# Attention keys split once and stored compactly; scores from four part products, 256 columns a pass

## The chip, the cores and the metric

The kernel runs on one core of a Trainium2 chip. The metric is the device time of one execution in microseconds. Engines: TensorE (PE, and PEld for its weight loads), VectorE (DVE), ScalarE (ACT), GpSimd (POOL) and SyncE (SP), which here only issues DMAs.

## What is computed

A residual stream `x` of 16 batches x 128 tokens x 256 passes through two blocks, each with a cross-attention to `ctx_2048` (same shape) and a feed-forward, each weighted by the tanh of a gate and fed by a layernorm without weights:

```python
x = x + tanh(g_xattn[0]) * L0_xattn(ctx, ctx, layernorm(x), ssm_kernel, D, 8)
x = x + tanh(g_ffn[0]) * L0_ffn(layernorm(x), ...)     # 8 shared units, 8 routed experts, top 2
x = x + tanh(g_xattn[1]) * L1_xattn(layernorm(x), ctx, ctx)
x = x + tanh(g_ffn[1]) * L1_ffn(layernorm(x), ...)     # 2 shared units, 32 routed experts, top 6
```

The change touches the third line. `L1_xattn` is causal softmax attention in each batch of 128 tokens, with 16 heads of 16 dimensions, scores `q k^T / 4`, and keys and values that are both slices of `ctx_2048`. All of it is fp32 in the reference.

## The kernel before

The program has four stages, and each engine has its own instruction queue that runs through them in order: `ctx` (the first cross-attention, a convolution), `f0` (the first feed-forward), `att` (the attention) and `f1` (the second feed-forward). Semaphores are set and awaited by hand.

**Precision.** TensorE runs most products in fp32r, a rounded fp32. Where more is needed an operand is split into a high part (a ScalarE copy that rounds) and a low part (the rest, a subtraction on VectorE or GpSimd), and the product is the sum of part products.

**Feed-forward (`feed_forward`, L167).** Two passes over the units, in half blocks of 512 tokens: K counts unit and half, 64 steps in `f0` (K < 16 shared, 16 to 31 routed, 32 to 47 shared, 48 to 63 routed). `h_prod(K + 1)` is 12 matmuls of 512 columns, `o_prod(K)` 6. Between them lie: hidden activation (ScalarE), the product with the gate rows of routed units (VectorE, L520) and with the second half (L525), `y_hi` (ScalarE, L444) and `y_lo` (VectorE, L308). SP runs its own loop over K in `sync`: `weights(K/2 + 4)` waits until unit K/2's weights are split, `gate_rows(K)` loads a row of gates to all partitions and waits until the slot of four routed steps before is free. At K = NK - 16 = 48 it calls `attention_loads` (6 key blocks, two constants, 2 value blocks). Over the last 12 steps `attention_ahead_act`, `_pe` and `_pool` prepare the first queries and keys.

**Attention.** A step n of 64 is a group of four heads: batch b = n // 4, group t = n % 4. The keys of a group are prepared on the host as a block diagonal of 128 rows x 512 columns (four heads, each 16 rows twice, and 128 keys), almost all of it zeros, in `k_blk`. `load_keys` brings one in (128 rows of 2 KB, ring of 6), `key_hi` and `key_lo` split it (ScalarE, GpSimd; ring of 4). Queries: `query_normed` normalizes a batch, `query_hi` and `query_lo` split it into `xn_split`, laid out so that one 128 x 128 transpose gives 64 rows of high and 64 rows of low parts of four heads; `query_turned` does four transposes (t = 3, for batch b + 2), `query_copy` scales and copies them to `q_split_t` (t = 0). `scores(n)` is three passes of 512 columns into one bank: the causal mask in bf16, query parts x high key block, query parts x low key block. VectorE takes the maxima (`maxima`) and subtracts them (`shifted`); `turned(n)` transposes the four heads (four transposes); ScalarE takes the exponential (`probs`); `values(n)` multiplies by the values with a column of ones. After each batch: `out_copy` (ScalarE), `out_rows` (four transposes, at t = 2 of the next), then `inverse`, `scaled`, `residual`, `moments` on VectorE.

TensorE's order in a step n (`c_tensor`) is `turned(n)`, `scores(n + 2)`, `values(n)`, then whatever is due. ScalarE's (`c_scalar`) is `out_copy` at t = 0, `probs(n)`, `query_copy` at t = 0, `key_hi(n + 4)`, `query_normed` at t = 2, `query_hi` at t = 3. GpSimd's (`c_gpsimd`): `key_lo(n + 4)`, `query_lo` at t = 3, and at n = 4 and 40 the `rstd` of the next norm. SP's (`c_sync`): the keys from n = 6 on, and behind the keys of n = 4m the values of batch m, which wait for `values` of step 4m - 5.

## Time and profile before

| | us |
|---|---|
| median of 3 runs (936.82 to 937.28) | 937.21 |
| profiled execution, its own time | 935.47 |
| its span, first to last instruction | 933.6 |
| PE busy | 898.5 (96%) |
| DVE busy | 603.4 (65%) |
| ACT busy | 551.0 (59%) |
| POOL busy | 202.4 (22%) |
| mean granted TensorE clock | 0.99 |

The chain of work that ended last is 88% TensorE: 37% the first products and 28% the second products of the feed-forwards (L646, L682). The attention lies between about 402 and 537 us. Times in rows are from the start of the span. A busy TensorE is not one at its peak, since the ends of its matmuls are modelled.

### The profile page before, as it was taken

Reading aid. Unit: us, or ns where it says so; the run is one execution under the profiler, and the core shown is the slowest. Engines: PE = TensorE matmul, PEld = TensorE weight load, DVE = VectorE, ACT = ScalarE, POOL = GpSimd, SP = SyncE. Lnnn points to the kernel's source line nnn. Section 1 sums busy time; section 2 is a strip of 40 time slices with the busy share of each in tenths; the row PEclk is TensorE's granted clock in tenths of the full one; section 3 lists DMA queues with packets and bytes.
Section 4 is the critical chain, followed back from the end, with each engine's and each line's share of the span. In section 5 each row is a group of like instructions: output and inputs, shape, how many; then the busy total and the mean of one; then the engine's idle time right before and its main releaser. Section 6 shows DMA issues by size and latency. Waiting matters only on the chain.

```text
span 933.6 us, 13901 instructions
## 1 busy us (share of the span) xinstructions
PE 898.5 (96%) x4704; PEld 719.5 (77%) x4704; DVE 603.4 (65%) x1390; ACT 551.0 (59%) x955; POOL 202.4 (22%) x172
## 2 busy tenths in 40 slices
PE   5899899999999999989999989999999999999998
PEld 5798788777788888856666667777788888888886
DVE  6678664465564566588888776566855466656654
ACT  3222343434444335468889677677777877777774
POOL 5899320000000012147777530000000000000000
PEclk9799999999999999999999999999999999999999
DMA  9101020333311351215554315434444244444443
GB/s 301 68 2 68 7 62 1 109 108 91 96 51 39 114 173 66 59 57 170 170 170 167 117 30 169 131 125 142 137 142 139 93 136 140 154 147 136 152 128 104
DMA packets 57957, 104.36 MB, mean 112 GB/s; under 512 B 7296, under 2 KB 13824, under 8 KB 57504
## 3 DMA queue, kind: packets, MB, share of 16 engines
q1 hardware_dynamic: 57168, 103.34, 34.5%
q8 instruction: 38, 0.62, 0.3%
q14 instruction: 31, 0.25, 0.1%
q10 hardware_dynamic: 720, 0.14, 0.1%
HBM read 101.03 MB, written 2.42 MB: 111 GB/s over the span
## 4 chain that ended last, share of the span: by engine, by line
PE 88%; DVE 5%; ACT 2%; POOL 1%; issue 1%; DMA 1%; SPq 1%; DVEq 0%; ACTq 0%; POOLq 0%
PE bank L646 37%; PE bank L682 28%; PE bank L1426 3%; PE bank L1437 2%; PE bank L1111 2%; PE bank L1113 2%; PE bank L1114 2%; PE bank L1126 2%; PE bank L1419 1%; PE bank L1418 1%; PE bank L350 1%; PE bank L1414 1%; PE bank L332 1%; DMA toeplitz<-in_kpad 1%; PE bank L1446 1%
## 5 line engine op out<-in xcount | busy, mean ns | idle before, releaser
L444 ACT ACTIVATE y_hi<-y 128x512 fp32r<-128x512 f32 x200 | 124.1, 621 | 82.2 <-DVE y L525 81.6
L539 DVE TENSOR_TENSOR y<-y,gate_rows 128x512 f32<-128x512 f32 x124 | 85.7, 691 | 120.6 <-ACT y L433 118.2
L682 PE MATMUL bank<-y_hi,w_hi 128*128 128x512 f32 x400 | 157.0, 393 | 1.5 <-DVE y_lo L308 1.0
L682 PE MATMUL bank<-y_lo,w_hi 128*128 128x512 f32 x400 | 156.5, 391 | 0.0
L682 PE MATMUL bank<-y_hi,w_lo 128*128 128x512 f32 x400 | 155.9, 390 | 0.0
L308 DVE TENSOR_TENSOR y_lo<-y,y_hi 128x512 fp32r<-128x512 f32 x196 | 134.3, 686 | 30.0 <-ACT y_hi L444 29.6
L427 ACT ACTIVATE activated<-bank 128x512 f32<-128x512 f32 x136 | 81.3, 597 | 80.9 <-PE bank L646 76.2
L646 PE MATMUL bank<-x_hi_first,w_hi 128*128 128x512 f32 x264 | 106.2, 402 | 0.7 <-DVE w_lo L303 0.7
L646 PE MATMUL bank<-x_hi_first,w_lo 128*128 128x512 f32 x264 | 104.2, 395 | 0.0
L646 PE MATMUL bank<-x_lo_first,w_hi 128*128 128x512 f32 x264 | 104.1, 394 | 0.0
L646 PE MATMUL bank<-x_hi_last,w_hi 128*128 128x512 f32 x264 | 103.9, 394 | 0.0
L646 PE MATMUL bank<-x_hi_last,w_lo 128*128 128x512 f32 x264 | 102.9, 390 | 0.0
L646 PE MATMUL bank<-x_lo_last,w_hi 128*128 128x512 f32 x264 | 102.7, 389 | 0.0
L1303 POOL TENSOR_TENSOR k_blocks_lo<-k_blocks_sb,k_blocks_hi 128x512 fp32r<-128x512 f32 x64 | 82.0, 1282 | 59.5 <-ACT k_blocks_hi L1299 59.0
L682 PEld LDWEIGHTS bank<-y_hi,w_hi 128*128 128x128 f32 x400 | 75.0, 188 | 20.4 <-DVE y_lo L308 2.9
L433 ACT ACTIVATE y<-activated 128x512 f32<-128x512 f32 x136 | 86.0, 632 | 4.3
L682 PEld LDWEIGHTS bank<-y_hi,w_lo 128*128 128x128 f32 x400 | 75.1, 188 | 16.3
L682 PEld LDWEIGHTS bank<-y_lo,w_hi 128*128 128x128 f32 x400 | 75.1, 188 | 16.2
L425 ACT ACTIVATE activated<-bank 128x512 f32<-128x512 f32 x64 | 38.3, 598 | 78.8 <-PE bank L646 78.8
L303 DVE TENSOR_TENSOR w_lo<-w_raw,w_hi 128x512 fp32r<-128x512 f32 (+1 forms) x96 | 75.1, 782 | 10.8 <-ACT w_hi L299 4.9
L299 ACT ACTIVATE w_hi<-w_raw 128x512 fp32r<-128x512 f32 (+1 forms) x100 | 69.7, 697 | 12.5 <-PE bank L682 12.5
L646 PEld LDWEIGHTS bank<-x_hi_first,w_hi 128*128 128x128 f32 x264 | 49.5, 188 | 12.5 <-DVE w_lo L303 1.0
(153 smaller groups left out, 1474.2 us busy)
## 6 DMA issues: line engine op xcount, KB each, us to landing
gate_rows<-gates SPq DMA_DIRECT2D x156, 256.0 KB, 3.7
w_raw<-in_wu SPq DMA_DIRECT2D x68, 256.0 KB, 2.6
k_blocks_sb<-in_k_blk SPq DMA_DIRECT2D x64, 256.0 KB, 4.2
w_raw<-in_wu SPq DMA_DIRECT2D x32, 384.0 KB, 3.1
v_slot<-in_v_rows SPq DMA_DIRECT2D x16, 256.0 KB, 2.6
ctx_windows<-in_ctx_win SPq DMA_DIRECT2D x3, 1024.0 KB, 11.8
toeplitz<-in_kpad SPq DMA_DIRECT2D x4, 512.0 KB, 8.7
X<-in_x SPq DMA_DIRECT2D x4, 512.0 KB, 9.2
```

The source lines that it names most:

```text
L299: act.activation(mem.whi[:, Nu % S, 0:WC], mem.wraw[:, Nu % S, 0:WC], ACT.Copy).then_inc(s_wh, 1)
L303: eng.tensor_tensor(mem.wlo[:, Nu % S, 0:WC], mem.wraw[:, Nu % S, 0:WC], mem.whi[:, Nu % S, 0:WC].bitcast(F32), ALU.subtract).then_inc(s_w ...
L308: eng.tensor_tensor(mem.ylo[:, K % S, :], mem.y[:, K % S, :], mem.yhi[:, K % S, :].bitcast(F32), ALU.subtract).then_inc(s_yl, 1)
L425: act.activation(mem.r[:, K % S, :], bk(2 * K % 3), ACT.Silu).then_inc(s_ac, 1)
L427: act.activation(mem.r[:, K % S, :], bk(K % 3), ACT.Relu).then_inc(s_ac, 1)
L433: act.activation(mem.y[:, K % S, :], mem.r[:, K % S, :], ACT.Square).then_inc(s_sq, 1)
L444: act.activation(mem.yhi[:, K % S, :], mem.y[:, K % S, :], ACT.Copy).then_inc(s_yh, 1)
L539: dve.tensor_tensor(mem.y[:, K % S, :], mem.y[:, K % S, :], gate, ALU.mult).then_inc(s_yd, 1)
L646: last = pe.matmul(o, w_[:, Nu % S, wc], x_[p][:, c, xs], start=(m == 0), stop=(m == 5))
L682: last = pe.matmul(acc(s)[:, c, :], w_[:, Nu % S, wc], y_[:, K % S, :], start=(n == 0 and m == 0), stop=(n == U - 1 and m == 2), skip_grou ...
L1303: pool.tensor_tensor(K2[:, n % KR, :], KM[:, n % KLR, :], K1[:, n % KR, :].bitcast(F32), ALU.subtract).then_inc(s_k2, 1)
L1426: last = pe.transpose(turn_bank(n)[:, g * P:(g + 1) * P], Ds[:, n % DR, g, :], ident[:])
```

## The change

Keys no longer come as zero-padded blocks. The host gives them compactly (`k_rows`: a batch is 128 rows x 256 columns). During `f0`, eight times (two batches at a time) `load_raw` brings them into the value buffer (SP, at K = 16, 18, then behind each store), `split_hi` (ScalarE, K = 19, 22 ... 40) and `split_lo` (GpSimd) split them into `xn_split`'s buffer, and `store_parts` (SP, K = 21, 24 ... 42) writes both parts with four DMAs to an internal DRAM tensor `k_parts`: for each batch 8 groups of 16 high and 16 low rows, each with two heads side by side (256 columns of 4 bytes).

For the attention a ring of 8 blocks (128 x 512) is cleared once on GpSimd (`blocks_zeroed`). `load_keys(n)` fills the two diagonal quarters of a block: for each half, one DMA reads 32 rows of `k_parts` twice (a step of 0 over a count of 2) into 64 partitions x 1 KB. The key blocks are used as they come; `key_hi` and `key_lo` are gone from the attention.

The query split is laid out with each high part and each low part twice, so that a head has 64 rows (high, high, low, low against high, low, high, low of the key), and 128 rows hold two heads. A batch therefore needs eight transposes in two groups (`query_turned(b, a)`, now of fp32r data with an fp32r identity, at t = 3 and at the next t = 0) and two `query_copy`, each placed ahead of `probs` at t = 0 and t = 1. `scores(n)` is the causal pass and two passes of 256 columns. In `f0`'s last steps there are four query groups instead of two, at K = 52, 55, 58, 61, and copies at K = 54, 57, 60, 63.

```diff
-                    if not final and K == NK - 16:
-                        attention_loads(sp)
+                    if not final:
+                        if K in (16, 18):
+                            load_raw(sp, (K - 16) // 2)
+                        if 21 <= K < 45 and K % 3 == 0:
+                            i = (K - 21) // 3
+                            store_parts(sp, i)
+                            if i + 2 < NB // 2:
+                                load_raw(sp, i + 2)
+                        if K == NK - 16:
+                            attention_loads(sp)
...
+                    for i in range(NB // 2):
+                        split_lo(pool, i)
+                    blocks_zeroed(pool)
...
+                        if 19 <= K < 43 and K % 3 == 1:
+                            split_hi(act, (K - 19) // 3)
                         attention_ahead_act(act, NK - K)
...
-        KLR, KR, SR, DR, PR = 6, 4, 3, 3, 3
+        KR, SR, DR, PR = 8, 3, 3, 3
         NQ = 4 * NB
         causal = sb("causal", [P, 4, P], BF16)
         identb = sb("identb", [P, P], BF16)
-        KM = sb("k_blocks_sb", [P, KLR, 4 * P])
-        K1 = sb("k_blocks_hi", [P, KR, 4 * P], F32R)
-        K2 = sb("k_blocks_lo", [P, KR, 4 * P], F32R)
+        K1 = sb("k_blocks", [P, KR, 4 * P], F32R)
+        ident_r = sb("ident_r", [P, P], F32R)
+        xc = sb("xn_c", [P, 2, D])
         V = sb("v_slot", [P, 2, NH1, 32])
-        xc = sb("xn_c", [P, 2, D])
-        xs = sb("xn_split", [P, 2, 4, 2, 64], F32R)
-        Q1 = sb("q_split_t", [P, 2, 4, P], F32R)
+        xs = sb("xn_split", [P, 2, 4, 2, P], F32R)
+        Q1 = sb("q_split_t", [P, 2, 2, 4, P], F32R)
...
+        def split_places(i):
+            parts = xs[:, i % 2].rearrange("p t a f -> p (t a f)")
+            return V[:, i % 2].rearrange("p h d -> p (h d)"), parts[:, 0:2 * D], parts[:, 2 * D:4 * D]
+
+        def load_raw(sp, i):
+            if i >= 2:
+                sp.wait_ge(s_k2, i - 1)
+            sp.dma_start(split_places(i)[0].rearrange("p (b f) -> p b f", b=2),
+                         k_rows[2 * i:2 * i + 2].rearrange("b p f -> p b f")).then_inc(s_kr[i % 2], 16)
+
+        def split_hi(act, i):
+            act.wait_ge(s_kr[i % 2], 16 * (i // 2 + 1))
+            if i >= 2:
+                act.wait_ge(s_ks[i % 2], 64 * (i // 2))
+            raw, high, _ = split_places(i)
+            act.activation(high, raw, ACT.Copy).then_inc(s_k1, 1)
+
+        def split_lo(pool, i):
+            pool.wait_ge(s_k1, i + 1)
+            raw, high, low = split_places(i)
+            pool.tensor_tensor(low, raw, high.bitcast(F32), ALU.subtract).then_inc(s_k2, 1)
+
+        def store_parts(sp, i):
+            sp.wait_ge(s_k1, i + 1)
+            sp.wait_ge(s_k2, i + 1)
+            for part, rows in enumerate(split_places(i)[1:]):
+                for j in range(2):
+                    place = k_parts[2 * i + j].rearrange("(g s d) f -> g s d f", s=2, d=HD1)[:, part]
+                    sp.dma_start(place, rows[:, j * D:(j + 1) * D].bitcast(F32)).then_inc(s_ks[i % 2], 16)
+
+        def blocks_zeroed(pool):
+            pool.memset(K1[:].rearrange("p n f -> p (n f)").bitcast(F32), 0.0).then_inc(s_kz, 1)
+
         def load_keys(sp, n):
-            if n >= KLR:
-                sp.wait_ge(s_k2, n - KLR + 1)
-            sp.dma_start(KM[:, n % KLR, :], k_blk[n]).then_inc(s_kl[n % KLR], 16)
+            if n >= KR:
+                sp.wait_ge(s_s, n - KR + 1)
+            for hh in range(2):
+                first = k_parts.offset + (2 * P * (n // 4) + 64 * (n % 4) + 32 * hh) * D
+                place = bass.AP(k_parts.tensor, first, [[0, 2], [D, 2 * HD1], [1, D]])
+                sp.dma_start(K1[64 * hh:64 * hh + 64, n % KR, hh * D:hh * D + D].bitcast(F32), place).then_inc(s_kl[n % KR], 16)
...
-        def key_hi(act, n):
-            act.wait_ge(s_kl[n % KLR], LOADED + 16 * (n // KLR + 1))
-            if n >= KR:
-                act.wait_ge(s_s, n - KR + 1)
-            act.activation(K1[:, n % KR, :], KM[:, n % KLR, :], ACT.Copy).then_inc(s_k1, 1)
-
-        def key_lo(pool, n):
-            pool.wait_ge(s_k1, n + 1)
-            pool.tensor_tensor(K2[:, n % KR, :], KM[:, n % KLR, :], K1[:, n % KR, :].bitcast(F32),
-                               ALU.subtract).then_inc(s_k2, 1)
...
         def query_hi(act, b):
             act.wait_ge(s_n, b + 1)
             if b >= 2:
-                act.wait_ge(s_xt, b - 1)
-            act.activation(xs[:, b % 2, :, 0, :], xc[:, b % 2, :].rearrange("p (q f) -> p q f", q=4),
-                           ACT.Copy).then_inc(s_hi, 1)
+                act.wait_ge(s_xt, 2 * (b - 1))
+            else:
+                act.wait_ge(s_ks[b], 64 * (NB // 4))
+            act.activation(part_rows(b, 0), copies_of(xc[:, b % 2, :]), ACT.Copy).then_inc(s_hi, 1)
 
         def query_lo(pool, b):
             pool.wait_ge(s_hi, b + 1)
-            pool.tensor_tensor(xs[:, b % 2, :, 1, :], xc[:, b % 2, :].rearrange("p (q f) -> p q f", q=4),
-                               xs[:, b % 2, :, 0, :].bitcast(F32), ALU.subtract).then_inc(s_lo, 1)
-
-        def query_turned(pe, b):
+            pool.tensor_tensor(part_rows(b, 1), copies_of(xc[:, b % 2, :]), part_rows(b, 0).bitcast(F32),
+                               ALU.subtract).then_inc(s_lo, 1)
+
+        def query_turned(pe, b, a):
+            if b + a == 0:
+                pe.wait_ge(s_ir, 1)
             pe.wait_ge(s_lo, b + 1)
-            if b > 0:
-                pe.wait_ge(s_qt, b)
+            if b + a > 0:
+                pe.wait_ge(s_qt, 2 * b + a)
             for t in range(4):
-                last = pe.transpose(x_bank[:, t * P:(t + 1) * P],
-                                    xs[:, b % 2, t].rearrange("p s f -> p (s f)").bitcast(F32), ident[:])
+                last = pe.transpose(x_bank[:, t * P:(t + 1) * P].bitcast(F32R), xs[:, b % 2, t, a, :], ident_r[:])
             last.then_inc(s_xt, 1)
 
-        def query_copy(act, b):
-            act.wait_ge(s_xt, b + 1)
+        def query_copy(act, b, a):
+            act.wait_ge(s_xt, 2 * b + a + 1)
             if b >= 2:
                 act.wait_ge(s_s, 4 * (b - 1))
-            act.activation(Q1[:, b % 2].rearrange("p t q -> p (t q)"), x_bank, ACT.Copy, scale=SCALE1).then_inc(s_qt, 1)
+            act.activation(Q1[:, b % 2, a].rearrange("p t q -> p (t q)"), x_bank, ACT.Copy, scale=SCALE1).then_inc(s_qt, 1)
 
         def attention_loads(sp):
-            for n in range(KLR):
+            for i in range(2):
+                sp.wait_ge(s_ks[i], 64 * (NB // 4))
+            sp.wait_ge(s_kz, 1)
+            for n in range(KR):
...
-            if left in (12, 11, 4):
-                query_normed(act, {12: 0, 11: 1, 4: 2}[left])
-            if left in (11, 10, 3):
-                query_hi(act, {11: 0, 10: 1, 3: 2}[left])
-            if left in (9, 8, 7, 6):
-                key_hi(act, 9 - left)
-            if left in (6, 3):
-                query_copy(act, {6: 0, 3: 1}[left])
+            if left == 16:
+                act.activation(ident_r[:], ident[:], ACT.Copy).then_inc(s_ir, 1)
+            if left in (15, 13, 4):
+                query_normed(act, {15: 0, 13: 1, 4: 2}[left])
+            if left in (14, 12, 3):
+                query_hi(act, {14: 0, 12: 1, 3: 2}[left])
+            if left in (10, 7, 4, 1):
+                query_copy(act, (10 - left) // 6, (10 - left) // 3 % 2)
 
         def attention_ahead_pe(pe, left):
 
-            if left in (8, 5):
-                query_turned(pe, {8: 0, 5: 1}[left])
+            if left in (12, 9, 6, 3):
+                query_turned(pe, (12 - left) // 6, (12 - left) // 3 % 2)
 
         def attention_ahead_pool(pool):
             query_lo(pool, 0)
             query_lo(pool, 1)
...
-                pe.wait_ge(s_k2, n + 1)
+                pe.wait_ge(s_kl[n % KR], LOADED + 32 * (n // KR + 1))
                 if t == 0:
-                    pe.wait_ge(s_qt, b + 1)
-                pe.matmul(s_bank(n), Q1[:, b % 2, t, :], K1[:, n % KR, :], start=False, stop=False)
-                pe.matmul(s_bank(n), Q1[:, b % 2, t, :], K2[:, n % KR, :], start=False, stop=True).then_inc(s_s, 1)
+                    pe.wait_ge(s_qt, 2 * b + 2)
+                blocks = K1[:, n % KR, :].rearrange("p (h a k) -> p h a k", h=2, a=2)
+                for a in range(2):
+                    last = pe.matmul(s_bank(n)[:, a * 2 * P:(a + 1) * 2 * P], Q1[:, b % 2, a, t, :], blocks[:, :, a, :],
+                                     start=False, stop=(a == 1))
+                last.then_inc(s_s, 1)
...
-                        query_turned(pe, b + 2)
+                        query_turned(pe, b + 2, 0)
+                    if t == 0 and b > 0 and b + 1 < NB:
+                        query_turned(pe, b + 1, 1)
...
+                    if t < 2 and b > 0 and b + 1 < NB:
+                        query_copy(act, b + 1, t)
                     probs(n)
-                    if t == 0 and b > 0 and b + 1 < NB:
-                        query_copy(act, b + 1)
...
-    blocks = np.zeros((NB, 4, 2, 4, HD1, 4, P), np.float32)
-    for h in range(4):
-        blocks[:, :, :, h, :, h, :] = heads[:, :, None, h]
-    blocks = blocks.reshape(NB * 4, P, 4 * P)
+    keys = heads.reshape(NB, 4, 2, 2, HD1, P).transpose(0, 1, 3, 4, 2, 5).reshape(NB, P, D)
```

## Rows read from the trace of the kernel before

**Rows 1.** Stretches in us: busy time (count) of PE, PEld, DVE, ACT, POOL; clock; DMA.
```profile
240.00:280.00 40.00, 40.00 (x178) 32.53 (x177) 24.37 (x63) 20.41 (x32) 0.00 (x0) 1.00 0.20 63
460.00:480.00 20.00, 19.92 (x184) 13.10 (x177) 17.80 (x34) 16.58 (x33) 15.32 (x14) 1.00 0.55 179
```
**Rows 2.** Timeline of one step: start, duration, engine, operation, count, [idle before, releaser].
```profile
454.04 0.59 ACT L1338 ACTIVATE q_split_t<-bank 128x512 fp32r<-128x512 f32 x1
...
454.55 0.66 PE L1426 MATMUL bank<-ident,y 128*128 128x128 f32 x4
...
455.24 0.60 ACT L1567 ACTIVATE activated<-bank 128x512 f32<-128x512 f32 x1
455.26 0.19 PEld L1419 LDWEIGHTS bank<-k_blocks_lo,q_split_t 128*128 128x128 f32 x1
455.49 0.39 PE L1419 MATMUL bank<-k_blocks_lo,q_split_t 128*128 128x512 f32 x1
455.89 0.16 PEld L1437 LDWEIGHTS bank<-activated,v_slot 128*32 128x32 f32 x8 [0.44 <-ACT activated L1567]
...
456.25 0.14 PEld L1426 LDWEIGHTS bank<-ident,y 128*128 128x128 f32 x1 [0.20 <-issue]
```
**Rows 3.** Waits, 403 to 537 us: who for whom, total, times, longest.
```profile
PEld bank L1437 <- ACT activated L1567: 29.1, 62, 0.9
```
**Rows 4.** Timeline, from t = 3 to the next t = 0.
```profile
452.41 0.42 PEld L1330 LDWEIGHTS bank<-ident,xn_split 128*128 128x128 f32 x4 [0.20 <-issue]
452.41 0.66 PE L1330 MATMUL bank<-ident,xn_split 128*128 128x128 f32 x4
...
452.80 0.47 PEld L1426 LDWEIGHTS bank<-ident,y 128*128 128x128 f32 x4
...
453.54 0.60 ACT L1567 ACTIVATE activated<-bank 128x512 f32<-128x512 f32 x1 [0.23 <-PE bank L1426]
```
**Rows 5.** The page's costliest groups: the key subtraction.
```profile
L1303 POOL TENSOR_TENSOR k_blocks_lo<-k_blocks_sb,k_blocks_hi 128x512 fp32r<-128x512 f32 x64 | 82.0, 1282 | 59.5 <-ACT k_blocks_hi L1299 59.0
```
**Rows 6.** Timeline of POOL and PEld at n = 42, 43.
```profile
487.30 1.64 POOL L139 TENSOR_TENSOR rstd<-vpe,mhalf 128x8 f32<-128x8 f32 x1
...
490.57 0.19 PEld L1418 LDWEIGHTS bank<-k_blocks_hi,q_split_t 128*128 128x128 f32 x1 [0.58 <-POOL k_blocks_lo L1303]
```
**Rows 7.** Timeline of PE: the transposes of n = 40 and n = 48.
```profile
483.60 0.60 PE L1426 MATMUL bank<-ident,y 128*128 128x128 f32 x4
...
500.42 0.38 PE L1426 MATMUL bank<-ident,y 128*128 128x128 f32 x2
```
**Rows 8.** Timeline of ACT and PEld at the end of the first feed-forward.
```profile
399.31 2.54 ACT L451 ACTIVATE out_scaled<-bank,tg 128x512 f32<-128x512 f32 x4
...
401.91 0.86 PEld L232 LDWEIGHTS bank<-ident,out_scaled 128*128 128x128 f32 x8 [1.78 <-ACT out_scaled L451]
```
**Rows 9.** DMA issues: count, KB each, median us to landing.
```profile
gate_rows<-gates SPq DMA_DIRECT2D x156, 256.0 KB, 3.7
...
v_slot<-in_v_rows SPq DMA_DIRECT2D x16, 256.0 KB, 2.6
```
**Rows 10.** DMA from 15 to 19 us.
```profile
DMA packets 1398, 1.40 MB, mean 351 GB/s; under 512 B 41, under 2 KB 1396, under 8 KB 1396
```
**Rows 11.** Timeline of SP: the key loads of `attention_loads`.
```profile
319.98 2.97 SPq L1288 DMA_DIRECT2D k_blocks_sb<-in_k_blk  x6
```
**Rows 12.** Timeline at K = 48 and 49: `y_lo`, the gate product, the output matmul.
```profile
335.83 0.69 DVE L308 TENSOR_TENSOR y_lo<-y,y_hi 128x512 fp32r<-128x512 f32 x1
...
337.65 0.69 DVE L520 TENSOR_TENSOR y<-activated,gate_rows 128x512 f32<-128x512 f32 x1 [1.13 <-ACT activated L425]
...
338.18 0.39 PE L682 MATMUL bank<-y_hi,w_hi 128*128 128x512 f32 x1
```
**Rows 13.** Timeline of SP: the value load of batch 2.
```profile
412.68 0.33 SPq L1293 DMA_DIRECT2D v_slot<-in_v_rows  x1
```
**Rows 14.** Timeline of PE: the score matmul of step 63.
```profile
530.59 0.58 PE L1418 MATMUL bank<-k_blocks_hi,q_split_t 128*128 128x512 f32 x1
```

More of the change, by code:

```diff
@@ L1260, in build @@
         identb = sb("identb", [P, P], BF16)
-        KM = sb("k_blocks_sb", [P, KLR, 4 * P])
-        K1 = sb("k_blocks_hi", [P, KR, 4 * P], F32R)
-        K2 = sb("k_blocks_lo", [P, KR, 4 * P], F32R)
+        K1 = sb("k_blocks", [P, KR, 4 * P], F32R)
+        ident_r = sb("ident_r", [P, P], F32R)
+        xc = sb("xn_c", [P, 2, D])
         V = sb("v_slot", [P, 2, NH1, 32])
-        xc = sb("xn_c", [P, 2, D])
-        xs = sb("xn_split", [P, 2, 4, 2, 64], F32R)
-        Q1 = sb("q_split_t", [P, 2, 4, P], F32R)
+        xs = sb("xn_split", [P, 2, 4, 2, P], F32R)
+        Q1 = sb("q_split_t", [P, 2, 2, 4, P], F32R)
         mem.out_scaled = sb("out_scaled", [P, 2, 2, BLK])
         s_sh = shift_sems["c"][1]
-        s_kl = ctx.s_cq + ctx.s_cg[0:2]
-        s_vl = [ctx.s_cg[2], ctx.s_kt[0]]
+        s_kl = ctx.s_cq + ctx.s_cg + ctx.s_kt[0:1]
+        s_vl = ctx.s_kt[1:3]
         LOADED = 16
         s_cc = sem("c_causal_loaded")
+        s_kr = [sem(f"c_k_raw_loaded{i}") for i in range(2)]
         s_k1 = sem("c_k_hi_ready")
         s_k2 = sem("c_k_lo_ready")
+        s_ks = [sem(f"c_k_parts_stored{i}") for i in range(2)]
+        s_kz = sem("c_k_blocks_zeroed")
+        s_ir = sem("c_identity_rounded")
         s_n = sem("c_normed")
@@ L1311, in query_normed, with copies_of, part_rows @@
                            scale=rstd[:, b:b + 1]).then_inc(s_n, 1)
+        def copies_of(view):
+            return view.rearrange("p (g f) -> p g f", f=HD1).unsqueeze(2).broadcast_to((P, NH1, 2, HD1))
+        def part_rows(b, part):
+            return xs[:, b % 2].rearrange("p t a (h s d f) -> p (t a h) s d f", h=2, d=2, s=2)[:, :, part]
         def query_hi(act, b):
@@ L1366, in attention_ahead_pool @@
             query_lo(pool, 1)
-            for n in range(KR):
-                key_lo(pool, n)
             query_lo(pool, 2)
@@ L1490, in c_sync @@
             def c_sync(sp):
-                for n in range(KLR, NQ):
+                for n in range(KR, NQ):
                     load_keys(sp, n)
@@ L1554, in c_tensor @@
                     if n == 54:
-                        pe.wait_ge(s_qt, b + 2)
+                        pe.wait_ge(s_qt, 2 * b + 4)
                         f1.logits(pe, 0, x_bank)
@@ L1721 @@
     arrays = {
-        "x": x, "ctx_win": windows, "k_blk": blocks, "v_rows": values,
+        "x": x, "ctx_win": windows, "k_rows": keys, "v_rows": values,
         "g_x": a["g_xattn"], "g_f": a["g_ffn"], "kpad": kpad, "d_skip": a["L0_xattn_D"],
```

9 lines of the change are left out of this document (3 added, 6 removed).

## The prediction

> **What bounds the kernel now.** I read first the table of stretches: TensorE is busy in all of 240 to 280 us, in the first feed-forward, and in 19.9 of the 20 us from 460 to 480, in the attention [rows 1]. So a TensorE instruction added to the feed-forward is paid in full. In the attention the busy share misleads, and I went to the timeline of one step (n is a group of four heads of one batch; a step is `turned(n)`, `scores(n+2)`, `values(n)`). The four transposes start at 454.55 and end at 455.21; the exponential runs on ScalarE from 455.24 to 455.84; the weights of `values` load at 455.89; the next transposes load at 456.25 [rows 2]. 0.66 + 0.03 + 0.60 + 0.05 + 0.36 = 1.70 us, the whole step. The three score matmuls lie beside the exponential: the weights of `values` waited 0.44 us for ScalarE [rows 2], and did so 62 times, 29.1 us in all [rows 3]. The step is a loop between TensorE and ScalarE with the scores in its shadow. A further group of four transposes (a query transpose, or `out_rows`) is in the loop: 0.39 us from 452.41 to 452.80, and the next exponential 0.04 later behind the warm start, 0.43 [rows 4]. A block of four steps is 4 x 1.70 + 2 x 0.43 = 7.66.
>
> **The change part by part.**
> *Scores.* In each of 64 steps the second 512-column pass goes and two passes of 256 columns remain. Passes follow each other by 0.23 us (its weights load at 455.26, it starts at 455.49) [rows 2]. With weight loads of 0.19 before each half pass I get some 0.12 us less TensorE time a step. The cover is the exponential: `values` can't start before it ends, whatever the scores take. Gain in the loop: nothing; on the two score groups inside the feed-forward 0.1 each, 0.2 us.
> *Splitting.* 64 ScalarE copies and 64 GpSimd subtractions of 1.28 [rows 5] leave the attention; 8 of each, same size, enter the first feed-forward, where ScalarE is busy 20.4 us of 40 and GpSimd 0 [rows 1]: hidden. With them goes a stall: the `rstd` of 1.64 us at 487.30 stands before the key subtractions on GpSimd, and the weights of the scores at 490.57 wait 0.58 us for one [rows 6]. From 483.60 to 500.42 two blocks took 16.8 [rows 7] instead of 15.3: 1.5 us back, and nothing late behind it, since ScalarE has 0.6 us a step less.
> *Query transposes.* Two groups a block instead of one. In the feed-forward two more, 0.43 each: 0.9. In the loop at n = 4, 8 ... 56; n = 4 lies where VectorE's residual work sets the step and hides it, 13 remain. ScalarE copies each before its exponential. It starts 512-column operations 0.5 apart (453.54 [rows 4], 454.04 [rows 2]); the transposes end at 452.41 + 0.66 = 453.07, so the copy starts at 453.10 and the exponential at 453.58 instead of 453.54 [rows 4]; about the same at t = 1. So 0.43 + 0.07 = 0.50 a block, 13 x 0.50 = 6.5 us. The transposes are fp32r now, of which the trace has none: four loads as now 0.42 [rows 4], or at most four of 0.19 as in the score loads [rows 2], 0.76, which over 28 groups would be 9 us more. I take 0.42; the nearest row is a transpose of the same tile.
> *End of the feed-forward.* A query copy now stands behind the last y_hi, ahead of the table load; `out_scaled` runs from 399.31 for 2.54 without a gap, and the attention's first transposes wait for it until 401.91 [rows 8]. The copy's issue distance, 0.45, is paid in full.
> *SP's queue.* `store_parts(i)` holds SP at K = 21, 24 ... until ScalarE (at K = 19, 22 ...) and GpSimd are through; then come five DMAs of 0.3 to 0.5. Behind it wait gate rows and weights. By the code SP runs up to four units, some 16 us, ahead of VectorE; the wait takes about nine of it, and gate rows take 3.7 to land [rows 9]: some 2 to 3 us stay. Hidden, narrowly. In `attention_loads` SP issues 16 key DMAs instead of 6.
> *Key loads.* This term decides. Before, a load is 128 rows of 2 KB. Now a step has two loads of 64 rows of 1 KB; the source of each is written as 2 copies (step 0) of 32 rows, the destination as 64 partitions. With all sixteen engines full of rows that average 1.0 KB (1398 packets, 1.40 MB in 4 us) the rate is 351 GB/s [rows 10], 21.9 an engine, 47 ns a row. If the 64 rows go over sixteen engines, a load is 4 rows, 0.19 us. If a transfer is dealt out by its outermost count, source and destination have no larger common one than two: 32 rows on each of two engines, 1.50 us, and the second load of the step on the same two another 1.50. No load of before starts with so few, so the trace doesn't show which. I take two engines: the outermost 2 is the only cut that both sides share as they are written. A step then needs 3.0 us of two engines, against (7.66 + 0.50) / 4 = 2.04 of compute, and the key stream becomes the bound.
> The Trainium skill, page "DMA: Bandwidth & Descriptors", section "Why a DMA increments its semaphore by 16 and not by 1", says that the number of engines is the largest up to 16 that divides the slowest dimension of both patterns, and its table of rules warns that a leading zero-stride broadcast of c copies keeps a DMA on c engines. By that rule the sum is the one with two engines; without it, that of the even spread below. No run here shows it yet.
>
> **The sum with two engines**, in the time of the profiled run (935.47; the median is 937.21, 1.7 more).
> (a) `attention_loads` starts at 319.98 [rows 11]. First data 1.3 us later (a value load lands in 2.6 [rows 9], of which its 16 KB an engine are 0.75). 16 loads x 1.50 = 24.0, to 345.3; two value loads 1.5, gate rows of K = 49 0.75, landing 0.6: 348.1. VectorE wants them at 337.65; in the unit before, `y_lo` was ready at 336.52 and the output matmuls started at 338.18, so TensorE has 1.7 us to spare [rows 12]. Stall 348.1 - 337.65 - 1.7 = 8.8 us.
> (b) With 0.9 and 0.45 from above the attention starts 10.1 us later.
> (c) Key 8 is asked for early; key 9 stands in SP's queue behind the value load that waits for `values(3)`, now issued at 412.68 [rows 13]: 422.8 then, keys 0.35 later, first data 424.4. Keys 9 to 63: 110 loads x 1.50 = 165.0; 14 value loads x 0.75 = 10.5. Three keys (9 us) are queued at each such wait, so the two engines don't run dry. Key 63 lands at 424.4 + 175.5 + 0.6 = 600.5.
> (d) The score matmul of step 63 stands at 530.8 now (behind the causal one at 530.6) [rows 14]. What follows shifts by 69.7: 935.5 + 69.7 = 1005.2, and 1.7 for the median: 1006.9, call it 1007.
> Bounds of this case: the two engines may stream faster or slower than when all sixteen are full (47 ns taken, 44 to 54): 990 to 1030. TensorE idles a third of the stage and its granted clock, 1.00 in [rows 1], could fall to half; then a block needs at most 4 x (1.70 + 1.02) + 3 x 0.86 = 13.5 against the loads' 8 x 1.50 + 0.75 = 12.75, up to 10 us more, inside that range.
>
> **The rivals.**
> *Even spread.* The rows go over all engines; 6.5 + 0.9 + 0.45 - 1.5 - 0.2 = 6.1 us slower: 943 (939 to 950). For it: all loads so far are spread evenly (all sixteen full in [rows 10]). Against: none has this form. If the fp32r transposes are dearer, or gate rows come late behind the stores (K = 22, 28, 31), 950 to 960.
> *Faster, the other side.* The spread is even and the second score pass counts in full: 64 x 0.23 = 14.7 off, 1.5 for the stall, less 13 x 0.43 = 5.6, 0.9 and 0.45: 9.2 faster, 928. It decides from the point at which `values` waits for TensorE and not for the exponential. For it: TensorE busy 99.6%. Against: the loop closes at 1.70 without the scores.
> *The change doesn't do what it says.* It is meant to halve the key bytes; if the source were re-formed to 64 rows, the even spread holds, and its time.
>
> **How the numbers follow.** Two engines 0.75 (1007), even spread 0.16 (943), its dear form 0.04 (955), faster 0.05 (928). The likeliest's own range is 990 to 1030; to hold 8 in 10 the range must take in the even spread: 940 to 1030. 0.2% of 937 is 1.9 us, about what a measurement can tell from no change: faster 0.05, same 0.01, slower 0.94.
>
> **What would show it.** Two engines: keys landing 10 us or more after their issue, scores waiting for `k_blocks` loads, blocks 12.7 us long, VectorE waiting 10 us for gate rows at K = 49. Even spread: blocks of 8.17, `values` still waiting for the exponential some 60 times. Faster: steps under 1.65. Wrong beyond these: ScalarE late with its copies, or gate rows late at K = 22.

## The result, and the profile after

| | before | after |
|---|---|---|
| median, us | 937.02 (936.16 to 937.28) | 1011.81 (1010.85 to 1012.65) |
| profiled execution: span | 933.6 | 1010.9 |
| PE busy | 898.5 | 912.3 |
| ACT busy | 551.0 | 532.7 |
| POOL busy | 202.4 | 143.2 |
| mean granted TensorE clock | 0.99 | 0.97 |

The changed kernel is slower: the ratio is 1.080 (1.0781 to 1.0818), and 1007 had been forecast. ScalarE and GpSimd have less to do, as the change meant. Between the two profiled executions the end comes 77.3 us later; the medians are 74.8 us apart.

The page of the changed kernel: first the chain that ended last, by engine; then the group of score passes (count, busy us, mean ns, idle before and what ended it); then the value loads among the DMA issues (count, KB each, median us to landing).

```profile
PE 69%; DMA 14%; SPq 5%; DVE 4%; issue 3%; ACT 3%; POOL 1%; DVEq 0%; ACTq 0%; POOLq 0%
...
L1472 PE MATMUL bank<-k_blocks,q_split_t 128*128 128x256 f32 x128 | 35.5, 362 | 50.6 <-DMA k_blocks<-k_parts 50.4
...
v_slot<-in_v_rows SPq DMA_DIRECT2D x16, 256.0 KB, 7.8
```

A DMA share of 14% stands in the chain, and the score passes over the key blocks were preceded by 50.4 us of waiting for key loads. A value load lands in 7.8 us instead of 2.6 [rows 9]. The waits from 403 to 612 us (who for whom, total, times, longest) have the same behind GpSimd's wait for the next query split:

```profile
...
PEld bank L1472 <- DMA k_blocks<-k_parts: 71.7, 51, 2.3
DVE max L1651 <- PE bank L1472: 69.7, 52, 3.5
...
PE bank L1472 <- DMA k_blocks<-k_parts: 50.4, 46, 1.9
...
PEld bank L1492 <- ACT activated L1622: 5.4, 12, 0.9
```

In [rows 3] the weights of `values` waited 29.1 us in 62 waits for the exponential. Here it is 5.4 us in 12 waits: the loop from transposes to values is no longer what closes last. Now the DMA queues from 466 to 476 us:

```profile
DMA packets 437, 0.46 MB, mean 46 GB/s; under 512 B 14, under 2 KB 420, under 8 KB 436
...
q1 hardware_dynamic: 436, 0.45, 13.4%
```

13.4% of sixteen engines is 2.1 engines. Of the 420 packets under 2 KB 14 are under 512 B; the other 406 are rows of 1 KB. On two engines that is 203 each in 10 us, 49 ns a row, with one value load beside them; [rows 10] gave 47 ns with all sixteen full. SP's timeline shows the period of a batch, between two value loads 12.33 us (449.55 to 461.88) and 12.55 (461.88 to 474.43), with the key loads holding SP itself nearly all of that time:

```profile
449.55 1.04 SPq L1346 DMA_DIRECT2D v_slot<-in_v_rows  x1
450.65 11.19 SPq L1341 DMA_DIRECT2D k_blocks<-k_parts  x8
461.88 1.35 SPq L1346 DMA_DIRECT2D v_slot<-in_v_rows  x1
```

In the first feed-forward, the counterpart of [rows 11] and [rows 12]: the 16 key loads on SP, the two constants behind them, and the gate product of K = 49 (the one of K = 48 was at 336.23).

```profile
322.71 19.59 SPq L1341 DMA_DIRECT2D k_blocks<-k_parts  x16
342.34 1.80 SPq L1397 DMA_DIRECT2D causal<-in_causal_c  x1
...
345.67 0.37 SPq L385 DMA_DIRECT2D gate_rows<-gates  x1
...
353.09 0.69 DVE L534 TENSOR_TENSOR y<-activated,gate_rows 128x512 f32<-128x512 f32 x1 [13.91 <-issue]
...
355.95 0.29 PEld L696 LDWEIGHTS bank<-y_hi,w_hi 128*128 128x128 f32 x1 [11.29 <-DVE y_lo L309]
...
356.00:358.00 2.00, 2.00 (x5) 1.62 (x6) 1.79 (x3) 1.25 (x3) 0.00 (x0) 0.50 0.17 64
```

VectorE stood for 13.9 us, and TensorE waited 11.3 us for `y_lo` behind it. The last line is a stretch with the columns of [rows 1]: TensorE resumed at a granted clock of 0.50, and its first six matmuls took 2.7 us to the start of the seventh instead of 1.4.

Where the 77.3 us of span went can be read from three events. The value load of batch 2, which the first attention steps release, came at 428.86 instead of 412.68 [rows 13]: 16.2. The score passes of step 63 came at 607.36 instead of 530.59 [rows 14], so the attention took 178.5 from that load instead of 117.9: 60.6. From there to the end it was 403.5 instead of 403.0: 0.5.

The 16.2 us can be parted further by the `y_lo` of VectorE. The first of the feed-forward starts at 126.03 instead of 124.56, before the change has had anything to do: 1.5 us, which the trace of *No low pass* below, a variant of the kernel before, has too (125.99). That of K = 48 starts at 338.49 instead of 335.83, 1.2 us more, and that of K = 56 at 384.03 instead of 368.47: 12.9 us more, of which the stall at K = 49 is 12.5 (see *First ring with the copies inside*). The other 0.6 us fall behind it.

### The profile page after: what moved, and what is told of

Same layout as the page of the kernel before. It is cut to its first block, busy times and chain, and to the rows that moved or that the text cites. A ratio compares the mean times of both kernels' runs of the same rounds, so it can differ in the third digit from the quotient of the medians.

```text
span 1010.9 us, 14027 instructions
## 1 busy us (share of the span) xinstructions
PE 912.3 (90%) x4768; PEld 728.3 (72%) x4768; DVE 604.7 (60%) x1390; ACT 532.7 (53%) x916; POOL 143.2 (14%) x117
## 4 chain that ended last, share of the span: by engine, by line
PE 69%; DMA 14%; SPq 5%; DVE 4%; issue 3%; ACT 3%; POOL 1%; DVEq 0%; ACTq 0%; POOLq 0%
PE bank L660 32%; PE bank L696 25%; DMA k_blocks<-k_parts 12%; SPq L1341 4%; PE bank L1125 2%; PE bank L1127 2%; PE bank L1128 2%; PE bank L1140 1%; PE bank L351 1%; DMA gate_rows<-gates 1%; DMA toeplitz<-in_kpad 1%; PE bank L1472 1%; PE bank L333 1%; PE bank L233 1%; DVE y L539 0%
## 5 line engine op out<-in xcount | busy, mean ns | idle before, releaser
L696 PEld LDWEIGHTS bank<-y_hi,w_hi 128*128 128x128 f32 x400 | 75.3, 188 | 33.8 <-DVE y_lo L309 16.2
L696 PEld LDWEIGHTS bank<-y_hi,w_lo 128*128 128x128 f32 x400 | 75.4, 189 | 16.4
L1651 DVE TENSOR_REDUCE max<-bank 128x4 f32<-128x512 f32 x64 | 44.1, 690 | 69.7 <-PE bank L1472 69.7
L304 DVE TENSOR_TENSOR w_lo<-w_raw,w_hi 128x512 fp32r<-128x512 f32 (+1 forms) x96 | 75.1, 782 | 11.4 <-ACT w_hi L300 5.7
L1472 PE MATMUL bank<-k_blocks,q_split_t 128*128 128x256 f32 x128 | 35.5, 362 | 50.6 <-DMA k_blocks<-k_parts 50.4
L300 ACT ACTIVATE w_hi<-w_raw 128x512 fp32r<-128x512 f32 (+1 forms) x100 | 69.7, 697 | 18.1 <-PE bank L696 13.1
```

The lines of the kernel that those rows point to most:

```text
L300: act.activation(mem.whi[:, Nu % S, 0:WC], mem.wraw[:, Nu % S, 0:WC], ACT.Copy).then_inc(s_wh, 1)
L304: eng.tensor_tensor(mem.wlo[:, Nu % S, 0:WC], mem.wraw[:, Nu % S, 0:WC], mem.whi[:, Nu % S, 0:WC].bitcast(F32), ALU.subtract).then_inc(s_w ...
L696: last = pe.matmul(acc(s)[:, c, :], w_[:, Nu % S, wc], y_[:, K % S, :], start=(n == 0 and m == 0), stop=(n == U - 1 and m == 2), skip_grou ...
L1472: last = pe.matmul(s_bank(n)[:, a * 2 * P:(a + 1) * 2 * P], Q1[:, b % 2, a, t, :], blocks[:, :, a, :], start=False, stop=(a == 1))
L1651: dve.tensor_reduce(nmax[:, n % DR, :], s_bank(n).rearrange("p (h k) -> p h k", k=P), AX_X, ALU.max).then_inc(s_m, 1)
```

## The experiments

The first five test the cause, the outermost count of the key loads, in three forms and in two places. The next three test the exponential's shadow. The last four look for a version that is worth having and for what limits it. Each diff is against the kernel that the text names.

**Copies inside.** The change with each load's 32 rows outermost and the two copies inside. The destination is the same 64 partitions in order, so the two copies of a row are now neighbours, and the query layout follows.

```diff
-                place = bass.AP(k_parts.tensor, first, [[0, 2], [D, 2 * HD1], [1, D]])
+                place = bass.AP(k_parts.tensor, first, [[D, 2 * HD1], [0, 2], [1, D]])
...
-            return xs[:, b % 2].rearrange("p t a (h s d f) -> p (t a h) s d f", h=2, d=2, s=2)[:, :, part]
+            return xs[:, b % 2].rearrange("p t a (h s d c) -> p (t a h) s d c", h=2, s=2, c=2)[:, :, :, :, part]
```

> The changed kernel with the two copies of a key row side by side: the source of a key load is 32 rows x 2 copies (step 0) instead of 2 copies x 32 rows, and the query parts are laid out to match. Same number of loads, rows and bytes. Theory 'dealt out by the outermost count': the loads now go over sixteen engines, no wait for keys stays, blocks of four steps take 8.17 us, and the time is that of the even spread, 943 (939 to 950). Rival 'zero step or compact source is slow in itself' (repeated reads, or rows of 1 KB): stays at 1005 to 1015. Rival 'scores count in full': below 932.

Measured 941.44 us (940.46 to 942.37), ratio 1.0049 (1.0036 to 1.0062). The same bytes in the same number of DMAs cost 70 us less, only for the order of the two outer dimensions. No wait for a key load is left among the longer ones, and the weights of `values` wait for the exponential again. First such a row from 410 to 540 us, then SP's timeline:

```profile
PEld bank L1492 <- ACT activated L1622: 29.4, 61, 0.9
...
320.99 10.21 SPq L1341 DMA_DIRECT2D k_blocks<-k_parts  x16
```

16 loads now hold SP for 10.2 us, 0.64 each, against 1.22 each in the change. A value load lands in 2.6 us again.

**Real step instead of zero.** In the changed kernel the outermost dimension is a 2 *and* a step of zero. This version parts the two: high and low parts lie in separate regions of `k_parts`, each load reads 32 rows once (four loads a step), and the outermost count is still 2.

```diff
+            for i in range(4):
+                hh, copy = i // 2, i % 2
+                at = 64 * hh + 32 * copy
+                first = k_parts.offset + (2 * P * (n // 4) + 32 * (n % 4) + 16 * hh) * D
+                place = bass.AP(k_parts.tensor, first, [[P * D, 2], [D, HD1], [1, D]])
+                sp.dma_start(K1[at:at + 32, n % KR, hh * D:hh * D + D].bitcast(F32), place).then_inc(s_kl[n % KR], 16)
```

> The change, with each of a step's four loads of 32 key rows read once, without the step of zero: the source is two blocks of 32 heads-by-columns rows with a real step between them, so the outermost count stays 2; the part products' layout follows it. Theory (the outermost count deals a load out over the engines): two engines carry a load as in the change, 64 rows of 1 KB on each engine a step, so 1007 to 1018. Rival (it is the step of zero, the repeated reading, that confines the load): the loads spread over all engines and the time is 941 to 950, near that of the version with the copies inside.

Measured 1010.65 us (1008.94 to 1011.9), ratio 1.0789 (1.0773 to 1.0806). The repeated reading is not the cause; the outermost 2 is. Waits from 410 to 610 us:

```profile
PEld bank L1474 <- DMA k_blocks<-k_parts: 68.4, 51, 2.0
```

**Rows outermost, four loads.** The control for it: four loads of 32 rows, 32 outermost, nothing repeated, the layout of the change.

```diff
+                row = 64 * (n % 4) + 32 * hh
+                place = k_parts[n // 4, row:row + 32]
```

> The same four loads of 32 rows a step and the layout of the change, but each source written with its 32 rows outermost and nothing repeated. Theory (outermost count): spread over all 16 engines, no waits for keys, 941 to 952; above the version with the copies inside by at most what SP pays for issuing four loads a step instead of two (4 x 0.46 us = 1.85 us) and by what the first block's gate rows come later in the first feed-forward for that. Rival (many small loads of 32 rows are slow however written): over 990.

Measured 946.83 us (945.85 to 947.86), ratio 1.0104 (1.009 to 1.0117). Small loads as such are fine. Of the 5.4 us above the version with the copies inside, 3.9 fall at K = 49 by the traces (from the `y_lo` of K = 48 to that of K = 56 it is 36.9 us against 33.0), and these are SP's: 32 issues hold SP from 321.95 for 14.7 us, and VectorE waits 5 us for gate rows.

```profile
321.95 14.74 SPq L1343 DMA_DIRECT2D k_blocks<-k_parts  x32
...
343.44 0.69 DVE L534 TENSOR_TENSOR y<-activated,gate_rows 128x512 f32<-128x512 f32 x1 [5.01 <-issue]
```

**First ring by four loads.** The change, but the eight key blocks loaded in the feed-forward come by four evenly spread loads each; later ones as in the change.

> The changed kernel with only the 8 key blocks that are loaded during the first feed-forward brought in by four loads of 32 rows each (no repeated source, outermost count 32), the other 56 as in the change. Theory: the stall of some 14 us at the gate rows of K = 49 goes and the attention stays bound by its key stream: 998 (995 to 1001). Rival 'the stall is only SP's 16 more issues': SP now issues 32 loads there, the stall stays or grows, 1010 or more.

Measured 1000.95 us (999.89 to 1002.3), ratio 1.0684 (1.0669 to 1.0698). It took 11 us off, but not all of the stall: 32 issues held SP for 14.8 us, and VectorE still waited 4.9 at K = 49. To price the stall whole I made it again with two loads each:

**First ring with the copies inside.**

```diff
-                place = bass.AP(k_parts.tensor, first, [[0, 2], [D, 2 * HD1], [1, D]])
+                source = [[D, 2 * HD1], [0, 2], [1, D]] if n < KR else [[0, 2], [D, 2 * HD1], [1, D]]
+                place = bass.AP(k_parts.tensor, first, source)
```

(`part_rows` follows for the first two batches.)

> The change, but the 16 key loads issued inside the first feed-forward (the first eight key blocks) have the copies inside, outermost 32; all later ones are as in the change. It takes away the stall in the feed-forward alone. Theory (the change's loss is that stall, some 11 us for TensorE, and the key stream of the attention): 999 to 1002, VectorE not waiting for gate rows at K = 49, attention blocks still 12 to 13 us. Rival (most of the loss hangs on the feed-forward's stall): under 960.

Measured 997.71 us (997.38 to 1001.71), ratio 1.0662 (1.0644 to 1.068). SP's timeline, and VectorE at K = 49:

```profile
414.46 0.34 SPq L1347 DMA_DIRECT2D v_slot<-in_v_rows  x1
...
338.43 0.69 DVE L534 TENSOR_TENSOR y<-activated,gate_rows 128x512 f32<-128x512 f32 x1 [1.12 <-ACT activated L437]
```

The value load of batch 2 moved from 428.86 to 414.46, by 14.4 us, and the medians are 14.1 apart. Not all of it is the stall: the `y_lo` of K = 48, ahead of it, already starts at 336.61 instead of 338.49, 1.9 us earlier (1.3 of them stand before the feed-forward). So the stall cost 12.5 us by these two traces. The rest, 997.7 against 941.4, is the attention's key stream, 56 us.

**No low pass.** The kernel before without its second score pass; the scores leave out the low parts of the keys, everything else is as it was.

```diff
-                pe.matmul(s_bank(n), Q1[:, b % 2, t, :], K1[:, n % KR, :], start=False, stop=False)
-                pe.matmul(s_bank(n), Q1[:, b % 2, t, :], K2[:, n % KR, :], start=False, stop=True).then_inc(s_s, 1)
+                pe.matmul(s_bank(n), Q1[:, b % 2, t, :], K1[:, n % KR, :], start=False, stop=True).then_inc(s_s, 1)
```

> The kernel before without the second score pass (query parts x low key block); the low parts of the keys are still made, but left out of the scores. Theory 'scores lie in the shadow of the exponential': within 2 us of the kernel before (936 to 938). Rival 'a score pass counts in full': 64 x 0.23 = 14.7 us faster, 922.

Measured 936.19 us (934.8 to 937.85), ratio 0.9997 (0.9988 to 1.0006). 64 whole passes left out, and nothing gained: TensorE only waited longer, 41.9 us instead of 29.1 [rows 3], for the exponential (403 to 537 us).

```profile
PEld bank L1436 <- ACT activated L1566: 41.9, 62, 1.0
```

**Groups into the shadow, after and before.** Since a transpose group between `scores` and the next `turned` is in the loop, both versions issue the query transposes and `out_rows` ahead of `values(n)` for n = 4 to 47, in TensorE's wait: the first on the version with the copies inside, the second on the kernel before.

```diff
+                    if 4 <= n < 48:
+                        if t == 3 and b + 2 < NB:
+                            query_turned(pe, b + 2, 0)
+                        if t == 0 and b > 0 and b + 1 < NB:
+                            query_turned(pe, b + 1, 1)
+                        if t == 2 and b > 0:
+                            out_rows(pe, b - 1)
                     if n < NQ - 1:
                         values(pe, n)
```

> The first experiment's kernel with the query transposes and out_rows ahead of values(n) instead of behind it, for n = 4 to 47. Theory 'the loop is transposes, exponential, values, and TensorE is free beside the exponential': each of the three groups a block costs 0.10 to 0.15 instead of 0.43, blocks of 7.1 to 7.3 instead of 8.17, some 10 us less than the first experiment: 933. Rival 'TensorE's total work sets the step': no change against the first experiment.

> The kernel before, with the query transposes and the out_rows group of the turned steps issued ahead of the values matmuls in the attention steps, nothing else. Theory (these groups stand between the transposes and the exponential on the path, and ahead of the values they run in TensorE's wait): about 933, 0.3 to 0.5 us of each of 12 blocks less. Rival (ScalarE's exponentials set the step whatever TensorE does first): within 0.2% of 936.5.

With the copies inside: 934.41 us (933.54 to 934.79), ratio 0.9971 (0.9959 to 0.9983), 7.0 below the version it is made from; a block fell from 8.03 to 7.39. On the kernel before: 936.38 (934.28 to 937.53), ratio 0.9992 (0.9983 to 1.0001), and my expectation of 933 was wrong. Its timeline says why; the first line is from the block before, the others are one step with a query group:

```profile
451.29 0.63 ACT L1299 ACTIVATE k_blocks_hi<-k_blocks_sb 128x512 fp32r<-128x512 f32 x1 [1.58 <-DMA k_blocks_sb<-in_k_blk]
...
459.55 0.60 ACT L1574 ACTIVATE activated<-bank 128x512 f32<-128x512 f32 x1 [0.25 <-PE bank L1426]
...
459.79 0.39 PE L1419 MATMUL bank<-k_blocks_lo,q_split_t 128*128 128x512 f32 x1
459.80 0.59 PEld L1330 LDWEIGHTS bank<-ident,xn_split 128*128 128x128 f32 x4
...
460.55 0.16 PEld L1437 LDWEIGHTS bank<-activated,v_slot 128*32 128x32 f32 x8 [0.17 <-issue]
```

The exponential ended at 460.15 and the second 512-column pass at 460.18. TensorE had no time left over in the shadow, so the group adds nearly its 0.4 us behind the scores wherever it stands, and the values' weights load at 460.55. I had taken the weight queue's idle 0.44 us [rows 2] for free time of TensorE. Something was gained all the same: of the eight blocks from n = 8 to 40 four took 7.52 to 7.55 us instead of 7.68. The other four took 7.61 to 8.29 and used that up. In two of them (8.29 and 8.04) a step with the query group was 0.5 to 0.8 us longer than in the others; in the first of these, `key_hi` waited 1.58 us for its key load (the first line) and the exponential stood behind it on ScalarE. Late keys come back below, when `values` moves. In the version with the copies inside the scores end at 456.72 and the exponential at 456.99: the change's shorter scores are worth nothing by themselves, but they make room for this reorder.

**Copies of the first queries earlier.** On the version with both, the four query groups of the feed-forward at 12, 10, 8, 6 steps before its end and their copies one step behind each.

> The version with the copies inside and the transposes ahead of the values, and in the first feed-forward the four query groups at 12, 10, 8 and 6 steps before its end instead of at 12, 9, 6 and 3, with the copies one step behind each, so that none stands behind the last y_hi. Theory (that copy's 0.45 us is on the path to the first out_scaled): 934.0, 0.45 below the version without it. Rival (it was hidden): the same 934.4.

Measured 933.94 us (933.0 to 934.48), ratio 0.9967 (0.9956 to 0.9979): 0.5 lower, as expected, but with overlapping spreads, so no more than likely.

**Values one step later.** The version with the copies inside and those earlier copies, and `values(n - 1)` in the place of `values(n)` for n = 5 to 48. `out_copy` goes behind `probs`.

```diff
-                    if n < NQ - 1:
-                        values(pe, n)
+                    if n != 4 and n < NQ - 1:
+                        values(pe, n - 1 if 4 < n <= 48 else n)
+                    if n == 48:
+                        values(pe, n)
```

> The version with the copies inside, the first query copies put earlier, and the values of a step issued one step later, so that the exponential leaves the loop from transposes to values. Theory: VectorE's maxima and copies, about 7.1 us a block, bound the step, 928 to 932. Rival: TensorE, now with 32 instead of 16 fp32 columns of scores per head in its way and no wait left, is the bound at about 7.3 to 7.5 a block: 933 to 936.

Measured 927.42 us (926.77 to 927.76), ratio 0.9896 (0.9882 to 0.9909): the fastest of all, 9.5 us below the kernel before. A bare step (transposes at 431.13, next at 432.53) takes 1.40 instead of 1.70, a block 6.7. Three stretches of its attention, columns as in [rows 1]:

```profile
420.00:440.00 20.00, 20.00 (x217) 15.56 (x217) 18.93 (x37) 14.62 (x28) 3.90 (x3) 1.00 0.35 104
440.00:460.00 20.00, 20.00 (x216) 15.36 (x215) 18.94 (x36) 14.69 (x27) 3.90 (x3) 1.00 0.39 117
460.00:480.00 20.00, 18.58 (x199) 14.17 (x196) 19.42 (x46) 14.40 (x27) 5.69 (x4) 1.00 0.37 113
```

In the first two TensorE is busy throughout by its modelled ends, which speaks for the rival, but a block takes less than the 7.3 to 7.5 us it gave; VectorE, with 18.9 of 20, is close behind, and in the third it is the busier of the two. The time is just below the range of the theory. Which of the two engines bounds the step no run here tells.

**The same on the kernel before.** Twice: as it is, and with each value load five key loads later in SP's queue.

```diff
-                    if n % 4 == 0 and n // 4 >= 2:
-                        load_values(sp, n // 4)
+                    if n % 4 == 1 and n // 4 >= 3:
+                        load_values(sp, n // 4 - 1)
+                load_values(sp, NB - 1)
```

> The kernel before with the values of a step issued one step later and the copy of o_t behind the exponential, as in the version that reached 927.4 us. It tells whether the scores' second 512-column pass costs time once nothing waits for the exponential. Theory (TensorE is then the bound, and the second pass, 0.23 us a step, counts): a block takes 6.71 us in that version; here 4 x 0.23 more for the passes, and less than it by one query group of 0.43 a block: 7.2 a block against 7.68 before, some 12 blocks, so about 931 (929 to 934). Rival (ScalarE or GpSimd, which split the keys here too, set the step): 7.7 a block, within 0.2% of before.

> The kernel before with the values one step later, as in the last version of it, and each value load put five key loads later in SP's queue, so that no key load stands behind the wait for a value slot. In the last version the value load waited one step longer (issued 8.5 us apart) and held back the four key loads behind it; the keys' low parts then came late from GpSimd (weights of the scores waited 16.7 us for them). Theory (that queue order alone cost the gain, and TensorE bounds the step with the second pass in it): blocks of 7.1 to 7.3 us, 929 to 934; above the change's version with late values, 927.4, by the 0.23 us of second pass a step less the second query group of a block. Rival (splitting the keys inside the attention is itself too slow for shorter steps, on ScalarE or GpSimd): blocks of 7.5 or more, 935 or above.

Measured 948.1 us (946.67 to 949.27), ratio 1.0122 (1.0108 to 1.0136), and 939.22 (938.1 to 939.5), ratio 1.0025 (1.0016 to 1.0034). Both theories fell; the second version came out where its rival had it, 935 or above. In the first, TensorE now waited for the keys' low parts, first row; with the queue mended this was half, second row (both from 410 to 550 us):

```profile
PEld bank L1418 <- POOL k_blocks_lo L1303: 16.7, 23, 1.2
...
PEld bank L1418 <- POOL k_blocks_lo L1303: 8.0, 12, 1.2
```

The wait for the value slot held four key loads behind it; 8.9 us of the 11.4 lost came back with the order of SP's queue. But a block still took 7.80, with TensorE busy 19.5 of 20 by its modelled ends. A bare step takes 1.62 there, 0.22 more than the 1.40 above. The difference lies in the scores: from their first weights to those of `values` it is 0.76 us here (last two lines) and 0.54 in the change's form (first two).

```profile
431.63 0.41 PEld L1472 LDWEIGHTS bank<-k_blocks,q_split_t 128*128 128x128 f32 x2
432.17 0.16 PEld L1492 LDWEIGHTS bank<-activated,v_slot 128*32 128x32 f32 x8
...
440.69 0.19 PEld L1418 LDWEIGHTS bank<-k_blocks_hi,q_split_t 128*128 128x128 f32 x1
...
441.45 0.16 PEld L1437 LDWEIGHTS bank<-activated,v_slot 128*32 128x32 f32 x8 [0.36 <-issue]
```

So the second pass is no longer hidden, by this reading; no run leaves it out here. The block is 0.5 us above 4 x 1.62 + 2 x 0.41 = 7.3, and about as much is one wait: once a block the weights of the scores come 0.56 late, behind GpSimd's subtraction, which comes behind ScalarE's `key_hi`, which comes behind `probs`, `query_copy` and `out_copy`. No run takes this wait away.

## Why the prediction was right

**Two engines.** The step that decided held, and its numbers with it. 47 ns a row: 49. 12.75 us a batch: eleven periods from 449.55 to 587.53, of 12.5 on average, nine of them 12.3 to 12.6. From the value load of batch 2 to the score passes of step 63: 177.7 forecast, 178.5 measured. The page "DMA: Bandwidth & Descriptors" of the Trainium skill, section "Why a DMA increments its semaphore by 16 and not by 1", had said that a transfer gets the largest number of engines, up to 16, that divides the slowest dimension of both patterns; the runs with 2 outermost (zero step or real) and with 32 outermost agree with it, 1011 against 941 and 947. Its warning in the table of rules, of an outermost dimension under 16, names the zero step as an example; the run without one agrees that it is not needed for the effect.

**The feed-forward's stall (a)** was a term with the wrong size: 8.8 us forecast, 12.5 measured. It counted the landing of the gate rows from the two engines' backlog as 348.1, with SP starting its loads at 319.98. SP began at 322.71, by which the same sum gives 350.8, and the product ran at 353.09, 2.3 us later still. The loads held SP for 19.6 us, 1.22 each where [rows 11] have 0.5, and the constant after them for 1.8, so the gate rows were issued only at 345.67; how much of the 2.3 us that explains no run tells. And the sum had no term for the clock behind the wait, which was at 0.50 and cost 1.4 us. Of the 7.6 us by which the shift was underestimated (77.3 against 69.7), the stall is 3.7. Another 1.5 stand before the first feed-forward and are none of the change's, 1.2 are the stores and splits (below), and 0.8 the attention; the rest is 0.5 or less a term, in both directions.

**The small terms (b)**: 1.35 us forecast. In the version without the stall the value load of batch 2 comes 1.8 us later than before (414.46 against 412.68). Of these 0.1 stand before the feed-forward, 0.7 come by K = 48, where the forecast had nothing, and 1.0 behind it, where (b) lies.

**The shadow of the exponential** held: a pass left out brings nothing (0.9997). The prediction left out its other half, which the reorders showed: before the change the scores fill the shadow to its end.

**Query transposes.** 0.50 a block more was forecast. With the copies inside the block is 8.03, 0.35 more than the 7.68 of before. The doubt on fp32r transposes ended on the cheap side: with an fp32r identity one takes 258 ns by its modelled end against 278 to 286 for fp32, and the next group's weights load 0.34 us behind the first of theirs (455.27 to 455.61 with the copies inside) instead of 0.39 [rows 4]. The even spread, forecast at 943, gave 941.4.

**The stores and the splits** were forecast as hidden, narrowly, and here the prediction was wrong by a little. Of the three steps that it named, K = 22, 28 and 31, the second came true. The lines are the product with the gate rows of K = 28 in the changed kernel, and a row of its waits from 205 to 320 us, which the kernel before hasn't got:

```profile
251.12 0.69 DVE L534 TENSOR_TENSOR y<-activated,gate_rows 128x512 f32<-128x512 f32 x1 [2.20 <-DMA gate_rows<-gates]
...
PEld bank L696 <- DVE y_lo L309: 1.5, 2, 1.3
```

Such waits of TensorE stand in the traces of all nine versions with the stores, 0.6 to 1.5 us together, and in none of the five of the kernel before and its variants. In that of the real step no product waits for gate rows there, and 0.6 us remain, so the late rows are not all of it; no run parts the stores from the splits.

**The stall by `rstd`** has no run of its own. Before, the two blocks from n = 40 took 16.8 us, 1.5 more than two others; with the copies inside they took 16.4, 0.4 more than two others there. So some 1.1 of the 1.5 us forecast came back.

**The clock.** In the key-bound attention TensorE idled a quarter to a third, and the granted clock fell for parts of it from its full level, 2.4 GHz, to half, 1.2; columns as in [rows 1]:

```profile
540.00:560.00 20.00, 15.08 (x115) 9.52 (x115) 11.01 (x21) 10.34 (x20) 1.36 (x2) 0.83 0.22 68
560.00:580.00 20.00, 14.21 (x126) 9.36 (x126) 12.26 (x21) 10.41 (x20) 2.56 (x2) 1.00 0.22 68
...
600.00:610.00 10.00, 7.55 (x44) 4.39 (x48) 4.06 (x7) 4.13 (x8) 2.08 (x2) 0.66 0.43 137
```

It can't have cost much: nine of the eleven periods of a batch are 12.3 to 12.6 us, some with a stretch at half clock and some without. The two longer ones, 13.24 and 12.86, had such a stretch too, and whether it made them longer no run tells.

## What to carry to other kernels

Write the long dimension of a DMA outermost on both sides: an outermost count of 2 confined a transfer to two engines, held the issuing queue as well, and cost 70 us here that one swap of two dimensions gave back. Find the loop that closes last before counting an instruction as a gain: 64 matmul passes were worth nothing while the exponential closed the loop, and by the timelines 0.22 us each once it was taken out, so shortening the covered work pays only together with a reorder that uses the room (927.4 against 936.9). When work is moved past a wait, look at what stands behind that wait in its queue, since a value load waiting one step longer starved the keys and cost 8.9 us. And look at what new work in the background delays, gate rows in a shared queue here: the splits and stores of the keys cost TensorE 0.6 to 1.5 us in every version that has them.

## What the hardware showed that I had not expected

- Issuing isn't free of the engines behind it: a key load held SP for 0.64 us when spread, 1.22 when on two engines in the feed-forward, and 1.40 (11.19 / 8) in the attention, nearly the 1.5 us that 32 rows on an engine take at 47 to 49 ns each (an estimate).
- A value load of 256 KB, spread over all engines, took 7.8 us to land while two were busy with key loads, and 2.6 in the version where the key loads were spread too.
- Transposes of fp32r data were cheaper than those of fp32, 258 against 285 ns by their modelled ends.
